# One transpose instead of four for the rough maxima of an attention kernel, and copies by quarters

## What is computed

```python
Q, K, V = query @ Wq + bq, key @ Wk + bk, value @ Wv + bv      # 8 key heads, 4 query heads to each, 16 wide
scores = jnp.einsum('bhgqd,bhkd->bhgqk', Q, K) * scale
w = jax.nn.softmax(scores, axis=-1)
y = jnp.einsum('bhgqk,bhkd->bhgqd', w, V)
x = x + y @ Wo + bo
h = relu(x_n @ up_w) ** 2                                       # x_n: x, normalised
x = x + layernorm(h @ down_w + routed(x_n)) * gamma + beta
```

## Time and profile before

| | us |
|---|---|
| median of 3 runs (lowest, highest) | 735.74 (735.54, 736.85) |
| the profiled execution | 734.63 |
| its span, first to last instruction | 732.8 |

### The profile page before, as it was taken

One profiled execution on the slowest core, in us unless ns is written; L12 is line 12 of the kernel. 1 busy time (PEld: TensorE's weight loads), 2 busy tenths in 40 slices (PEclk: granted clock), 3 DMA queues, 4 the chain that ended last, 5 costly groups with the idle time before them and its releaser, 6 DMA issues.

```text
span 732.8 us, 12481 instructions
## 1 busy us (share of the span) xinstructions
PE 681.9 (93%) x3952; PEld 491.7 (67%) x3952; DVE 494.6 (67%) x1125; ACT 503.4 (69%) x901; POOL 380.9 (52%) x465
## 2 busy tenths in 40 slices
PE   8689999999987989799999999999999999998894
PEld 3335556565553557577887878878878877876673
DVE  4578788887742876676776776777667767756412
ACT  3558787876723989678788687697787786885210
POOL 1447999987654232443652653553554545544333
PEclk9689999999997999999999999999999999999998
DMA  7224544362222120101101101101101101000000
GB/s 247 86 73 117 144 123 150 116 173 88 86 59 104 44 86 16 44 3 56 44 16 57 43 14 57 43 14 57 43 14 57 43 14 57 14 17 29 1 16 29
DMA packets 25783, 45.71 MB, mean 62 GB/s; under 512 B 3184, under 2 KB 4976, under 8 KB 25744
## 3 DMA queue, kind: packets, MB, share of 16 engines
q1 hardware_dynamic: 25744, 45.24, 19.6%
HBM read 36.84 MB, written 8.39 MB: 62 GB/s over the span
## 4 chain that ended last, share of the span: by engine, by line
PE 50%; ACT 16%; issue 11%; DVE 11%; POOL 10%; DMA 1%; POOLq 0%; DVEq 0%; ACTq 0%; SPq 0%
ACT x L422 6%; PE ps_b L1011 5%; ACT q_stack L422 5%; PE ps_b L1013 5%; PE ps_b L1012 5%; PE wide L1069 4%; PE ps_b L1049 4%; PE bank L1079 4%; PE ps_a L1049 4%; PE wide L1011 4%; PE wide L1013 3%; PE wide L1012 3%; POOL x_res L711 3%; DVE x_in L768 2%; POOL stage L688 2%
## 5 line engine op out<-in xcount | busy, mean ns | idle before, releaser
L422 ACT ACTIVATE q_stack<-qt_h 32x512 fp32r<-32x512 f32 x128 | 80.7, 631 | 1.9
L618 POOL TENSOR_TENSOR va<-mv,small 128x1 f32<-128x1 f32 x80 | 15.2, 190 | 126.3 <-DVE mv L991 78.7
L708 POOL TENSOR_TENSOR y_l<-y,y_h 128x512 fp32r<-128x512 f32 x16 | 20.6, 1287 | 110.6 <-ACT y_h L560 110.6
L1011 PE MATMUL ps_b<-down_h,ht_h 128*128 128x512 f32 x128 | 53.4, 417 | 3.4 <-DVE ht_l L955 2.7
L920 DVE RECIPROCAL y<-ps_b 128x256 f32<-128x256 f32 x32 | 55.9, 1748 | 0.0
L1011 PE MATMUL wide<-up_h,t_h 128*128 128x512 f32 x128 | 52.3, 408 | 1.2 <-DVE t_l L900 1.2
L1013 PE MATMUL wide<-up_h,t_l 128*128 128x512 f32 x128 | 50.6, 396 | 0.0
L1013 PE MATMUL ps_b<-down_h,ht_l 128*128 128x512 f32 x128 | 50.6, 395 | 0.0
L1012 PE MATMUL wide<-up_l,t_h 128*128 128x512 f32 x128 | 50.6, 395 | 0.0
L1012 PE MATMUL ps_b<-down_l,ht_h 128*128 128x512 f32 x128 | 50.5, 394 | 0.0
L620 POOL TENSOR_TENSOR rs<-va,small 128x1 f32<-128x1 f32 x80 | 43.9, 549 | 6.3
(11 more groups left out here) (203 smaller groups left out, 2180.6 us busy)
## 6 DMA issues: line engine op xcount, KB each, us to landing
x_in<-in_x SPq DMA_DIRECT2D x16, 256.0 KB, 2.7
ctx_t<-in_ctx SPq DMA_DIRECT2D x16, 256.0 KB, 2.7
x_res<-in_x SPq DMA_DIRECT2D x16, 256.0 KB, 2.7
x_in<-x_rows SPq DMA_DIRECT2D x16, 256.0 KB, 2.7
ctx_t<-in_ctx_turned SPq DMA_DIRECT2D x16, 256.0 KB, 2.9
x_res<-x_rows SPq DMA_DIRECT2D x16, 256.0 KB, 3.6
out<-stage SPq DMA_DIRECT2D x16, 256.0 KB, 2.0
x_rows<-x SPq DMA_DIRECT2D x8, 256.0 KB, 2.1
```

Of the source, the lines that this page charges most:

```text
L422: last = act.activation(out[STACK * part:STACK * (part + 1), p, :], halves[STACK * p:STACK * (p + 1), :].bitcast(F32), ACT.Copy)
L1011: pe.matmul(out_ps, w_hi, m_hi, start=start, stop=False)
```

## The change

`gmax` grows from 4 blocks of 8 columns to 4 blocks of 32 columns (`STACK`), one for each `b` and `n`, of which 8 are used; it is cleared once ahead of pass 2. PE turns the whole tile by one transpose of 128 columns, so that quarter (b, n) comes to lie in partitions 32(2b + n) and the seven behind it, in columns 0 to 127 of bank[1]. ACT still makes four copies of 8 x 512 elements, now one for each quarter: input 8 x 128 from partition 0, 32, 64 or 96, read once for each head pair, output in `q_stack` at partition 96 in blocks of 64 columns. Semaphores and their counts stay.

```diff
-        gmax = sb("gmax", [P, 2, 2, 2, PART])
+        gmax = sb("gmax", [P, 2, 2, STACK])
...
-                    for p in range(PAIRS):
-                        last = act.activation(q_stack[GUARD:GUARD + NKV, p, :], bank[1][0:NKV, :],
-                                              ACT.Copy, scale=-1.0)
+                    guards = q_stack[GUARD:GUARD + NKV].rearrange("h p (g b q) -> h p g b q", g=GROUPS, b=2)
+                    for b in range(2):
+                        for n in range(2):
+                            quarter = bank[1][STACK * (2 * b + n):STACK * (2 * b + n) + NKV, 0:P]
+                            last = act.activation(guards[:, :, 2 * n:2 * n + 2, b, :],
+                                                  quarter.rearrange("h (g q) -> h g q", g=2).unsqueeze(1)
+                                                  .to_broadcast([NKV, PAIRS, 2, SEQ]), ACT.Copy, scale=-1.0)
                     last.then_inc(S["ngm_s"], 1)
...
             dve.memset(vbd[:], 0.0).then_inc(S["vbd_zero"], 1)
+            dve.memset(gmax[:], 0.0)
...
-                    dve.tensor_reduce(gmax[:, b, :, r, :],
+                    dve.tensor_reduce(gmax[:, b, :, PART * r:PART * (r + 1)],
...
                     pe.wait_ge(S["gmax_s"], 4 * t + 4)
-                    turned = bank[1][0:NKV].rearrange("h (g b q) -> h b g q", g=GROUPS, b=2)
-                    for b in range(2):
-                        for n in range(2):
-                            last = pe.transpose(turned[:, b, 2 * n:2 * n + 2, :],
-                                                gmax[:, b, n].rearrange("p r h -> p (r h)"), ident)
-                    last.then_inc(S["gmt_ps"], 1)
+                    pe.transpose(bank[1][:, 0:P], gmax[:].rearrange("p b n h -> p (b n h)"), ident).then_inc(S["gmt_ps"], 1)
```

## The result

The change made the kernel slower, and by more than was forecast: 744.1 us median (6 runs, 741.37 to 745.72) beside 736.39 for the kernel before, a ratio of 1.0105 (95% interval 1.0083 to 1.0127). The forecast was 739.6 us. The profiled execution (743.99 us) has a span of 742.2 us, 9.4 more than before.

The account below looks back on a forecast made before the run. A ring of waits through PE, DVE, POOL and ACT was taken to bound the kernel, not PE's time. 12 x 0.25 = 3.0 plus 3 x 0.31 = 0.9 gave +3.9 us, so 739.6 us; range 737.3 to 741.8.

Parts of the forecast that it names:

- the period: Time of one turn of the ring in steady state, 28.17 us, predicted to become 28.42 us.
- ACT's branch: ACT's x_h and four copies, which must end before PE's scores; claimed to come last, with 0.06 us of slack.
- The slack of 0.06 us: Scores' load to first product behind the scores: 0.64 us in the steady tile against 0.58 in tile 2.
- PE: One transpose instead of four saves PE 0.25 or 0.33 us per tile; claimed worth 0 while ACT's branch is last.
- Rival 5: PE is the bound after all: 12 tiles save 0.33 us each, 4.0 less, 731.8 us; chance 0.04.
- ACT: ACT's four copies per tile lose their overlap as start partitions change: 2.33 us instead of 2.02, 0.31 more per tile.
- rival 4: ACT's copies lose overlap and each lasts 0.03 us longer: 1.8 on top of the forecast, 741.4 us; chance 0.10.
- The start of the copies: ACT's first copy still starts 0.63 us after x_h starts: gain 0, with 0.12 us as the bound.
- Rival 3: ACT's copies lose overlap but start earlier, by 0.12 us: +2.1, 737.9 us; chance 0.08.
- rivals 1 and 2: ACT's copies keep overlap: 1, start unchanged, 735.0 us, chance 0.10; 2, start 0.12 us earlier, 733.2 us, chance 0.06.
- DVE: One memset ahead of the second pass, at most 0.27 us, hidden by 2.49 us of DVE's idle time.
- the ring: Loop of waits through PE, DVE, POOL and ACT in each second-pass iteration; claimed to bound it, 28.17 us.

Follow-up runs that it names:

- e1: The changed kernel with its one transpose of the maxima made four times over: 744.88 us median, ratio 1.0113 to the kernel before.
- e2: The changed kernel's one transpose alone, with ACT's copies as before, all from partition 0: 739.23 us median, ratio 1.0035.
- e6: The kernel before with a fifth, small unused copy on ACT ahead of the four: 739.33 us median, ratio 1.0026.
- e3: The kernel before with ACT's copies cut by quarters as in the change, all from partition 0: 735.70 us median, ratio 1.0004.
- e9: The changed kernel with extra filling matmuls on PE in iterations -3 to -1 and 14: 739.12 us median, ratio 1.0037.
- e12: The changed kernel run once more, unaltered: 743.51 us median, ratio 1.0094 to the kernel before.
- e5: The kernel before with 20 filling matmuls on PE in iteration -1: 735.24 us median, ratio 0.9974.
- e4: The changed kernel with 20 filling matmuls on PE in iteration -1: 741.75 us median, ratio 1.0072 to the kernel before.
- e7: The changed kernel with the fourth quarter copied by DVE and three by ACT: 732.77 us median, ratio 0.9954 to the kernel before.
- e10: e7 with DVE and ACT counting up one semaphore, so PE waits once: 730.28 us median, ratio 0.9927 to the kernel before.

## Why the prediction was wrong

**What bounds the kernel.** Right. e1 gave PE 0.33 us per tile back and the period did not move; e2 took 0.33 from PE and won 0.06 to 0.07; e6 lengthened ACT's branch by 0.17 and the period grew by 0.10. The slack of 0.06 us, read as the difference of two distances in the trace, was right to 0.01.

**PE.** Right: worth nothing behind ACT's branch. DVE's sum behind the down projection comes 0.31 us earlier after L1033 (3.65 instead of 3.96) and changes nothing. Rival 5 is excluded, and tile 15 costs nothing: there the scores' load comes 2.67 us after the down projection's first, 2.68 before.

**ACT.** The mechanism was right, the size a little low: 2.39 us instead of 2.33. The term that was mis-sized is the single copy: the sum kept 574 ns, and it is 589. The 574 were a mean over a series in which three of four copies overlap, and an overlapping copy is recorded shorter (569 ns in e6). I had put a longer copy down to the form of its output or input (rival 4); e3 has that form and 573 ns. A steady tile grew by 0.31 to 0.32 us instead of 0.25, a tile of the start by 0.37 instead of 0.31.

**The start of the copies.** Right: 0.63 us after x_h, with the maxima ready earlier. Rival 3 falls with it, and rivals 1 and 2 fall with the lost overlap.

**DVE.** Nothing shows at the memset: the copies of tile 0 start at 247.80 before and at 247.82 after.

**The sum.** The step that failed is one that it put at nothing without a reason: that PE's granted clock stays what it was. The runs showed a fall to the lower level around tile 2 that costs 4.3 us in the profiled pair. The 9.4 us of that pair are 3 x 0.37 = 1.1 for the copies of tiles 0 to 2, 4.3 for the lower clock between 297 and 311 us, and 3.9 for the 12 turns of the ring (tile 3's copies are 5.43 us late, tile 15's load 9.31). So the ring alone is 5.0, inside the range, where 3.9 was forecast; the clock took the time out of it. In e9's profile, which has the same ring without that stretch, the tiles from 3 on start 4.6 us earlier, of which it has 0.4 from pass 1. The prediction read the granted clock in the steady part (1.00) and took it for the whole second pass. It quoted PE's idle time of 2.76 us at tile 2 without asking what the clock does around it, and it gave the range half a us for the spread of the runs.

**What is open.** Why the change makes the fall so frequent. Both parts do it alone: e2 (the one transpose only) had a mean clock of 0.971 or less in eight of 12 runs, e1 (the copies only) 0.970 in four of six. Before, eleven of 82 runs were above 738 us; since e3 took 737.8 with the fall, the true share may be larger. What PE does right ahead of the place does not tell the two kernels apart. Counted back 20 us from the first product behind x3 (296.02 and 296.81), PE is busy 16.77 us with 113 products in both, and its wait for x3 is 2.32 and 2.33 us. One falls and the other doesn't. The longer wait for the copies (3.19 us instead of 2.49) comes only after the first fall, ahead of the second stretch. The kernel before falls at times by itself; what tips it in a given run was not found. That filling takes the fall away is shown (e9 against e12, and less sharply e5 against before); that the four slower runs of e4 lost their clock in the last tiles, as the second profile of the changed kernel does, is only likely, since none of them was profiled.

## What to carry to other kernels

A saving on the busiest engine is worth what the ring leaves of it: look where two branches meet, and measure the slack from the end of the last producer to the start of the consumer, in a tile where the consumer was free and in one where it wasn't. Before a small step is handed to another layout, ask what it does to the overlap of short instructions on the engine that pays for it, and don't price a copy without overlap by the mean of copies that have it. And where PE idles near the start of a phase, its clock may fall in one run and not in the next. Look at the clock of the stretches with idle time, not only at that of the steady part, and in more than one run. When you compare such a stretch in two kernels, take the same place of the program and not the same time: from 290 to 297 us PE is busy 4.37 us before and 3.94 after, and 0.79 us earlier it is 3.94 in the kernel before too.

## What the runs showed of the hardware

Copies of 8 x 512 elements on ACT overlap by 0.09 us when all go from partition 0 to partition 96 (before, e3), and have a gap of 0.012 us and last 15 ns longer when the source's start goes from 0 to 32, 64 and 96 (573 and 589 ns, the changed kernel). The Trainium skill ("ScalarE: Activation LUTs", section "What ACT_TABLE_LOAD costs") gives an overlap of about 93 ns; the runs agree for the first case and not for the second.

Each semaphore wait that PE has to pass between the last copy and the load of its weights costs 0.11 us. In tiles 0 and 1, before and after, none stands behind the one for ngm_s (the helper leaves out the wait for relu_s as long as it is for 0 or less), and the load comes 0.11 us after the last copy. From tile 2 on relu_s stands there, and it is mostly 0.21 to 0.22. In e7, with ngd_s as well, it is 0.22 and 0.32 to 0.33. The trace's own records of these waits lie 0.106 us apart (536.265 and 536.371 in the changed kernel, with the load at 536.447).

e10 has 0.11 us in tiles 0 and 1 and 0.22 in tiles 2 and 3, as that rule has it, but 0.07 to 0.08 from tile 5 on, in the hardware loop. There the trace has the records of the other waits at 521.25 and 521.45, ahead of the copies' end, and the wait for ngm_s is on the load itself, so nothing stands between. Why the program comes out in that order in the loop was not looked into.
